# A gated attention and feed-forward layer: most of the second product's partial results are added into their sums by accumulating DMAs instead of by GpSimd

## What is computed

```python
# x, ctx: (16, 128, 1024) float32; weights are 4-bit integers in int32, one scale and zero for each group of 128
x = x + tanh(g_xattn) * window_attention(layernorm(x), ctx)      # 8 heads, window of 16
gate = silu(layernorm(x) @ dequant(gate_w))                      # (2048 rows, 1024) @ (1024, 3584)
up   = layernorm(x) @ dequant(up_w)
out  = x + tanh(g_ffn) * ((gate * up) @ dequant(down_w))         # (2048, 3584) @ (3584, 1024)
```

## Time and profile before

| | |
|---|---|
| median of 3 runs | 1661.05 us (1656.76 to 1664.93) |
| the profiled execution | 1667.74 us, span 1665.9 us |
| PE busy | 1574.3 us, 95% of the span |
| DVE busy | 1517.5 us, 91% |
| POOL busy | 1452.7 us, 87%; of that 792.6 us in L602 |
| ACT busy | 990.1 us, 59% |
| DMA | 166.66 MB, mean 100 GB/s |
| mean granted clock of TensorE | 0.986 |

### The profile page before, as it was taken

The page is one execution under the profiler, slowest core; times in us unless marked ns, Lnnn a source line. Parts: engine busy times, 40 slices in busy tenths (PEclk is TensorE's granted clock), DMA queues, the critical chain, the costliest instruction groups (busy, mean ns, idle before and its releaser), DMA issues.

```text
span 1665.9 us, 40474 instructions
## 1 busy us (share of the span) xinstructions
PE 1574.3 (95%) x16614; PEld 805.3 (48%) x16614; DVE 1517.5 (91%) x1483; ACT 990.1 (59%) x1133; POOL 1452.7 (87%) x891
## 2 busy tenths in 40 slices
PE   6898999897889999999999999999999999999996
PEld 3566667575533444444444444444444444444444
DVE  5687878776689999999999999999999999999997
ACT  4677778676445555555555555555555555555552
POOL 4576777676688999999999999999999999999975
PEclk9899999999899999999999999999999999999999
DMA  5655666655332222222222222222222222222128
GB/s 123 162 142 141 169 150 149 150 142 136 104 105 64 76 76 77 76 77 76 77 76 77 76 75 78 74 76 70 75 75 76 77 76 77 76 76 76 39 101 303
DMA packets 169522, 166.66 MB, mean 100 GB/s; under 512 B 11918, under 2 KB 135502, under 8 KB 169322
## 3 DMA queue, kind: packets, MB, share of 16 engines
q1 hardware_dynamic: 168186, 163.74, 34.9%
q10 hardware_dynamic: 1152, 0.33, 0.1%
HBM read 113.92 MB, written 16.78 MB: 78 GB/s over the span
## 4 chain that ended last, share of the span: by engine, by line
PE 84%; issue 5%; POOL 4%; DVE 3%; DMA 1%; ACT 1%; SPq 1%; ACTq 0%; DVEq 0%; POOLq 0%
PE bank L1168 63%; PE bank L1077 4%; PE bank L1066 3%; PE bank L1109 2%; POOL oacc L602 2%; DVE acc L950 2%; PE bank L1029 2%; PE bank L1040 2%; PE bank L1025 2%; PE bank L1033 2%; PE bank L1087 1%; PE bank L1056 1%; PE bank L1037 1%; PE bank L1045 1%; POOL raw_z L541 1%
## 5 line engine op out<-in xcount | busy, mean ns | idle before, releaser
L950 DVE SCALAR_TENSOR_TENSOR acc<-bank,scale,acc 128x1024 f32<-128x1024 f32 x784 | 950.5, 1272 | 13.7 <-PE bank L1168 8.9
L1168 PE MATMUL bank<-xT,w_int 128*128 128x512 f16 x3584 | 847.9, 380 | 13.2 <-ACT d_part L787 5.2
L602 POOL TENSOR_TENSOR oacc<-oacc,d_part 128x1024 f32<-128x1024 f32 x335 | 792.6, 2366 | 34.3 <-ACT d_part L787 19.1
L787 ACT ACTIVATE d_part<-bank,scale 128x1024 f32<-128x1024 f32 x335 | 372.7, 1113 | 379.9 <-PE bank L1168 373.3
L1168 PEld LDWEIGHTS bank<-xT,w_int 128*128 128x128 f16 x3584 | 349.5, 98 | 439.7 <-DVE acc L950 8.5
L1168 PE MATMUL bank<-h_hi,d_int 128*128 128x512 f16 x896 | 340.2, 380 | 9.0 <-ACT acc L767 2.5
L1168 PE MATMUL bank<-h_lo,d_int 128*128 128x512 f16 x896 | 339.5, 379 | 0.0
L541 POOL TENSOR_TENSOR raw_z<-raw_w,raw_z 128x512 int32<-128x512 int32 x168 | 264.1, 1573 | 9.0 <-DMA raw_z<-in_L_ffn_gate_z_dram 5.3
L1168 PEld LDWEIGHTS bank<-h_hi,d_int 128*128 128x128 f16 x896 | 87.4, 98 | 148.4 <-DVE acc L950 26.2
L974 DVE SCALAR_TENSOR_TENSOR oacc<-bank,scale,oacc 128x1024 f32<-128x1024 f32 x113 | 143.8, 1273 | 0.8 <-PE bank L1168 0.8
L668 ACT ACTIVATE pT<-bank 96x1024 f16<-96x1024 f16 x128 | 123.6, 1018 | 34.2 <-PE bank L1077 33.8
(11 more groups left out here) (84 smaller groups left out, 1377.2 us busy)
## 6 DMA issues: line engine op xcount, KB each, us to landing
raw_w<-in_L_ffn_gate_w_dram SPq DMA_DIRECT2D x56, 256.0 KB, 3.0
raw_z<-in_L_ffn_gate_z_dram SPq DMA_DIRECT2D x56, 256.0 KB, 3.7
raw_w<-in_L_ffn_up_w_dram SPq DMA_DIRECT2D x56, 256.0 KB, 3.0
raw_z<-in_L_ffn_up_z_dram SPq DMA_DIRECT2D x56, 256.0 KB, 3.7
raw_w<-in_L_ffn_down_w_dram SPq DMA_DIRECT2D x56, 256.0 KB, 2.7
raw_z<-in_L_ffn_down_z_dram SPq DMA_DIRECT2D x56, 256.0 KB, 3.4
vt<-vn_hl SPq DMA_DIRECT2D x64, 192.0 KB
vt<-vn_hl SPq DMA_DIRECT2D x64, 160.0 KB
```

The source lines that it names most:

```text
L602: nc.gpsimd.tensor_tensor(into, into, part, ALU.add).then_inc(d_added, 1)
L787: nc.scalar.activation(d_part[:, (count(c, x, False) - 1) % 2, :], pair[slot][:, :, :].rearrange("p h r -> p (h r)"), ACT.Copy, scale=scal ...
L950: nc.vector.scalar_tensor_tensor(out=into, in0=pair[u % 4][:, :, :].rearrange("p h r -> p (h r)"), scalar=scale[:, par, i, m, k:k + 1], in ...
L1168: last = nc.tensor.matmul(dst[:, h, :], weights, rows_of(h, part), start=(part == 0), stop=(part == 1))
```

## The change

ACT scales into one of four buffers instead of two. POOL no longer adds: it issues a DMA from its own queue that reads the buffer and accumulates it into the tile of oacc (accum_op add, SBUF to SBUF, 512 KB). There is one semaphore for each buffer, raised by 16 when its DMA has landed. POOL doesn't wait for its addition before any more, but for the landing of the one into the same tile. ACT waits for the landing four before. DVE's additions and the final transposes wait for landings where they waited for d_added. Which units are DVE's is unchanged.

```diff
+    NPART = 4
...
+        d_more = sb("d_more", [P, NPART - 2, TB], fp32)
+        d_parts = [d_part[:, n, :] for n in range(2)] + [d_more[:, n, :] for n in range(NPART - 2)]
...
+        d_added = [sem(f"d_added{n}") for n in range(NPART)]
...
+        def d_landed(n):
+
+            return d_added[(n - 1) % NPART], 16 * ((n - 1) // NPART + 1)
...
             def add_down(c, x):
                 n = count(c, x, False)
                 pool.wait_ge(d_scaled, n)
-                if n > 1:
-                    pool.wait_ge(d_added, n - 1)
-                else:
+                if n == 1:
                     pool.wait_ge(oacc_zeroed, NCT)
                 cc, xx = ahead(c, x)
                 if cc >= 0 and taken_by_dve(cc, xx):
                     pool.wait_ge(d_summed, count(cc, xx, True))
-                part = d_part[:, (count(c, x, False) - 1) % 2, :]
+                elif cc >= 0:
+                    pool.wait_ge(*d_landed(count(cc, xx, False)))
+                part = d_parts[(n - 1) % NPART]
                 into = oacc[:, x % NCT, x // NCT // SC % NT, :]
-                nc.gpsimd.tensor_tensor(into, into, part, ALU.add).then_inc(d_added, 1)
+                nc.gpsimd.dma_start(into, part, accum_op=ALU.add).then_inc(d_landed(n)[0], 16)
...
             def scale_down(c, x, par, slot):
                 n = count(c, x, False)
                 act.wait_ge(down_ready, c * NQT * NCT + x + 1)
-                if not isinstance(n, int) or n > 2:
-                    act.wait_ge(d_added, n - 2)
-                nc.scalar.activation(d_part[:, (count(c, x, False) - 1) % 2, :],
+                if n > NPART:
+                    act.wait_ge(*d_landed(n - NPART))
+                nc.scalar.activation(d_parts[(n - 1) % NPART],
...
                 if cc >= 0 and not taken_by_dve(cc, xx):
-                    dve.wait_ge(d_added, count(cc, xx, False))
+                    dve.wait_ge(*d_landed(count(cc, xx, False)))
...
                 if b == 0:
                     x = SC * NCT - 1
                     pe.wait_ge(d_summed, count(NC - 1, x, True))
-                    pe.wait_ge(d_added, count(NC - 1, x, False))
+                    for n in range(NPART):
+                        pe.wait_ge(*d_landed(count(NC - 1, x, False) - n))
...
                 x = NQT * NCT - NCT + ct_
-                pe.wait_ge(d_summed if x in LATE_DVE else d_added, count(NC - 1, x, x in LATE_DVE))
+                if x in LATE_DVE:
+                    pe.wait_ge(d_summed, count(NC - 1, x, True))
+                else:
+                    pe.wait_ge(*d_landed(count(NC - 1, x, False)))
```

More of the change, by code:

```diff
@@ L201, in flamingo_layer @@
             sem("h_hi_ready"), sem("h_lo_ready"))
-        down_ready, d_summed, d_scaled, d_added = (
-            sem("down_ready"), sem("d_summed"), sem("d_scaled"), sem("d_added"))
+        down_ready, d_summed, d_scaled = sem("down_ready"), sem("d_summed"), sem("d_scaled")
+        d_added = [sem(f"d_added{n}") for n in range(NPART)]
         row_back = [sem(f"rows_of_block{t}_back") for t in range(NT)]
```

## The result

The changed kernel takes 1676.74 us, median of 11 runs (1669.33 to 1688.13), against 1662.03 (1655.71 to 1667.56) for the kernel before: a ratio of 1.0104, 95% interval 1.0082 to 1.0125. It is slower by 1%. I had forecast 1726 us, slower by 3.9%. The direction held, the size did not: of 65 us of added time that I had forecast, 14.7 came.

What follows compares the result with a forecast made beforehand. DVE bounded by a hair, PE 0.33 us behind per quarter; after the change, the DMA engines. First quarters -5, steady quarters +55, tail +15 on 1667.7 us gave 1733, or 1726 for the median (6.7 lower); range 1644 to 1910.

Steps and rivals of the forecast that it cites:

- L957 is relieved: Steady quarters: without POOL's additions, DVE's L957 may take 1.22 us instead of 1.97; at worst POOL's subtraction still delays it.
- PE's 20.72 decides: Steady quarters: DVE then needs 20.3 us, so PE's 20.72 us sets the quarter, a gain of 17 us.
- POOL's issue: Steady quarters: each DMA issue occupies POOL 1 to 1.5 us, hidden behind PE, with room for 2.3 us each.
- The price of an accumulation: DMA engines: a 512 KB accumulation costs twice a copy, 2.71 us, with bounds of 1.35 and 4.06 us.
- The quarter of 22.1 us: Steady quarters: six accumulations plus weights' loads fill the DMA engines for 22.1 us against 21.05, costing +55 us; chance 0.42.
- My own sign of being wrong: Steady quarters: wrong if six accumulations take clearly less than 15 us of the DMA engines, or clearly more than 17.
- ACT's wait: Steady quarters: ACT's d_part waits on a landing from POOL's queue in every quarter; on PE alone if it fits.
- The first quarters: Before the steady part: of 13.6 us of stalls on d_part, 5 us are gained; bounds 0 and -13.6.
- The wait for a buffer: ACT with four buffers: some 9 us allowed, landings of 5.2 to 8.8 us, so hidden while the engines keep up.
- The weights: Weight loads: two accumulations in front are covered, a third makes a piece late; late weights or slow issue, chance 0.09.
- The tail: After 1629 us: seven accumulations lengthen the already full DMA engines' work by +15 us, bounds +7 and +28.
- it fits: Rival: accumulations take 2.5 us or less, PE's 20.72 bounds: 1646 to 1654, or 1661 to 1671 if L957 collides; chance 0.32.

Runs made afterwards that it cites:

- kernel 2: Against the changed kernel: POOL adds again everywhere except the seven last additions that are not DVE's, still accumulating DMAs; four buffers kept; 1690.08 us, ratio 1.0147.
- kernel 6: The changed kernel with two buffers instead of four, all its additions still by DMA; 1807.25 us, ratio 1.0864.
- kernel 9: Against the changed kernel: five of eight down units by DMA, one by POOL, two by DVE at places 2 and 7; tail on POOL; 1656.90 us, ratio 0.9970.
- kernel 10: As kernel 9, but DVE's two down units are at places 0 and 7 instead of 2 and 7; 1642.44 us, ratio 0.9888.
- kernel 11: Against the changed kernel: still six of eight by DMA, but DVE's units at places 0 and 7 and the tail on POOL; 1668.18 us, ratio 1.0040.
- kernel 1: The changed kernel with the seven last additions that are not DVE's put back on POOL; 1663.82 us, ratio 1.0012.
- kernel 8: Against the changed kernel: of eight down units DVE has one, POOL three, DMA four; tail on POOL; 1639.48 us, ratio 0.9855.

## Why the prediction was wrong

*L957 is relieved: right, in part by luck, and worth less than said.* It takes 1.21 us after, but not because the additions are gone: POOL's subtraction, which the prediction named as the bad case, can delay it as much (kernels 2 and 6). In the changed kernel POOL had no instruction under way in 53 of 56 cases. "PE's 20.72 decides" was wrong: DVE's sum over a quarter fits, its sum from unit 3 to 22 doesn't. The quarter became 21.00, a gain of 0.08 us in most of them and 3.4 us in all, not 17 (kernels 9 and 10).

*POOL's issue.* 1 to 1.5 us taken, some 0.9 measured: hidden.

*The price of an accumulation: right.* 2.71 us taken, 2.75 measured; by the packets, a 4 KB row takes 328 ns in the median where a copy's, from or to DRAM in this kernel, takes 159. The Trainium skill, "Collectives: The Full Stack" (The bandwidth ceiling: the fold count and why AG ≠ RS ≠ AR), says that an add's second source read halves the rate; the trace agrees by the medians: 328 / 159 is 2.06. The 2.1 us estimated from its rate was too low.

*The quarter of 22.1 us: the step that failed.* I added 16.2 us for accumulations and 5.9 for weights and held the sum against the clock as if a share of 1.00 were the limit. By measured prices the sum is 6 x 2.75 + 5.4 = 21.9 us of share, and all of it fits into 21.00 us: the share reads 1.04, in kernel 11 even 1.05, and 21.9 / 1.05 is 20.9. A share of 1.00 was no limit, since packets overlap in the records. They do so in one queue already: from 1645 to 1655 us of the kernel before, with SP's queue alone,

```profile
q1 hardware_dynamic: 3559, 3.85, 107.1%
```

So the six just fit under 21.00. The term of +55 us was in truth 0. It was mis-sized by 1.1 us a quarter, 5% of the sum, and that is nearly the whole error of the forecast. One accumulation more and the mechanism is there in full: +2.7 us a quarter with seven. My 22.1 came from choosing the higher of two shares for the weights, and rows 8 had already shown shares of 1.07. My own sign of being wrong, six accumulations well outside 15 to 17 us, did not speak: they took 16.5. The sign that did was the other one, ACT's wait: it stood on PE alone, as the prediction had it for the case that fits.

*The first quarters.* -5 taken, 0 measured. The gain is there (11 us at half width) and is given back to the DMA engines.

*The wait for a buffer: right.* Hidden with four buffers; with two it costs 130 us.

*The weights: right in kind.* With seven they are late by more than the buffers. The changed kernel is at that edge: landings of 7.5 us in the median for 10.5 allowed; with the same six, kernels 1 and 11 have single late pieces.

*The tail: right, and too small.* +15 taken, 7 to 28 as bounds, +20.5 measured. The seven accumulations make 17 to 18 of it (kernels 1 and 2). That is their work, 19 us less the 2 us left free, the sum from which I then took 2 us more off. The other 3.5 us come with the accumulations before the tail: with the tail on GpSimd it is 55.8 us with four of eight by DMA (kernel 8), 58.3 to 58.7 with five, 59.4 to 59.8 with six, 62.9 with seven, 64.4 with eight.

Of the rivals, "it fits" was the nearest for the quarter. Its first branch had the 17 us that did not come and ended below 1661. Its second had them stay away, 1661 to 1671 (by its own terms 1663 to 1671). Its condition was that L957 still collides, which it did not, and the kernel ended 6 us above it, by the tail.

## What to carry to other kernels

Add up the DMA engines' time for each stage, and treat an accumulating DMA as two copies; when the sum is within 5% of the stage, don't forecast a loss or a gain from the sum alone, but ask which transfer has the least slack: here the weights' landing. Look apart at stages in which the engines are already full: the seven accumulations of the tail cost 17 us, five times the 3.4 us that came with all the others. And relieving an engine pays only where its work lags locally: the same additions, moved by six units, gave 14 us.

## What the runs showed of the hardware

- An accumulation of 512 KB from SBUF to SBUF keeps the 16 engines 2.75 us, lands in 4.5 to 15.8 us (median 6.9) under this load, and its issue occupies POOL for 0.87 us.
- The DMA share read 1.04 in the steady part of the changed kernel with hardly anybody waiting. What marks the limit is the rate that no longer rises with the same mix of transfers: 225 and 229 GB/s with six, 219 with seven, 210 with eight.
- L957, with both operands in SBUF, and a POOL addition or subtraction, which read SBUF too, run one after the other: whichever began second ended 1.08 to 1.14 us after the first, in nearly all cases of all kernels. L957 took 1.97 us so the earlier trace rows, and 1.21 where POOL was idle. The Trainium skill, "SBUF — State Buffer" (Who interferes with whom), says that such an instruction contends with a GpSimd one that reads SBUF; the trace agrees.
